# One fused layer on one core: the same stages in another hand-written order

## The reference

```
x = x + retention(layernorm(x))          # per sequence, 8 heads
  q, k rotated; v, g = x @ wv, x @ wg
  qk = (qr @ kr.T) * decay_mask;  qk = qk / clip(abs(qk.sum(-1)), 1)
  out = qk @ v;  out = out * rsqrt(mean(out^2));  out = (silu(g) * out) @ wo
x = x + ffn(layernorm(x))                # here the 8 sequences are the "time" axis
  attention over the sequences at the same position, 16 heads, 4 key/value heads, causal
  h1 = x + ao @ wproj;  x2 = layernorm(h1)
  router: softmax over 8 experts, the best 2, with a capacity of 640 tokens for each expert
  each expert: gelu(x2 @ w1[e]) @ w2[e], weighted and added to h1
```

## Time and profile before

| | |
|---|---|
| median of 3 runs | 232.73 us (232.41 to 233.09) |
| time of the profiled execution | 232.53 us |
| its span | 230.7 us |
| PE busy | 218.4 us (95% of the span) |
| DVE busy | 180.6 us (78%) |
| ACT busy | 148.6 us (64%), of it 48.8 us in 38 table loads |
| POOL busy | 87.5 us (38%) |
| granted clock of PE | 1.0 throughout |

### The profile page before, as it was taken

One profiled execution on the slowest core, in us unless ns is written; L12 is line 12 of the kernel. 1 busy time (PEld: TensorE's weight loads), 2 busy tenths in 40 slices (PEclk: granted clock), 3 DMA queues, 4 the chain that ended last, 5 costly groups with the idle time before them and its releaser, 6 DMA issues.

```text
span 230.7 us, 5045 instructions
## 1 busy us (share of the span) xinstructions
PE 218.4 (95%) x1794; PEld 185.6 (80%) x1794; DVE 180.6 (78%) x549; ACT 148.6 (64%) x274; POOL 87.5 (38%) x107
## 2 busy tenths in 40 slices
PE   7898897999998999999999999999999799989994
PEld 7577675888976879878989788968897789878994
DVE  2799968898998899789988997897479846875533
ACT  3648757789856589648874886559656574737331
POOL 0000243235274436346455752653197317701000
DMA  5994000000000000000000000000000000000000
GB/s 160 298 323 104 1 3 1 3 0 0 4 0 4 0 26 0 1 3 1 23 3 0 3 1 26 0 0 12 15 0 4 23 0 3 23 0 1 26 0 23
DMA packets 8072, 6.45 MB, mean 28 GB/s; under 512 B 752, under 2 KB 7152, under 8 KB 8048
## 3 DMA queue, kind: packets, MB, share of 16 engines
q1 hardware_dynamic: 8048, 6.14, 9.1%
HBM read 5.09 MB, written 1.05 MB: 27 GB/s over the span
## 4 chain that ended last, share of the span: by engine, by line
PE 59%; issue 12%; DVE 11%; POOL 9%; ACT 6%; DMA 1%; DVEq 0%; POOLq 0%; ACTq 0%
PE bankm L860 15%; PE bankm L849 15%; POOL prodv L325 5%; PE bankf L672 3%; PE bank L739 3%; PE bankf L680 3%; PE bankf L731 3%; ACT L480 3%; POOL prod L317 3%; PE bank L761 2%; PE bank L787 2%; DVE ao L1058 2%; PE bank L770 2%; PE bankf L689 2%; PE bankf L700 1%
## 5 line engine op out<-in xcount | busy, mean ns | idle before, releaser
L849 PE MATMUL bankm<-x2T,w 128*128 128x256 f32 x256 | 64.9, 386 | 1.9 <-DVE res L1165 1.7
L860 PE MATMUL bankm<-w,hT 128*128 128x128 f32 x512 | 64.9, 276 | 0.1
L860 PEld LDWEIGHTS bankm<-w,hT 128*128 128x128 f32 x512 | 62.1, 192 | 2.0 <-issue 0.8
L1165 DVE SCALAR_TENSOR_TENSOR res<-bankm,gate,res 128x128 f32<-128x128 f32 x128 | 38.3, 341 | 21.3 <-PE bankm L860 20.7
L628 ACT ACTIVATE hT<-bankm 128x512 f32<-128x512 f32 x64 | 37.5, 596 | 26.7 <-PE bankm L849 26.5
L849 PEld LDWEIGHTS bankm<-x2T,w 128*128 128x128 f32 x256 | 45.2, 190 | 10.0 <-DVE res L1165 4.3
L480 ACT ACT_TABLE_LOAD x38 | 48.8, 1283 | 1.4 <-PEq L1207 0.7
L317 POOL TENSOR_TENSOR prod<-qkv 128x384 f32<-128x384 f32 (+5 forms) x12 | 19.9, 1681 | 18.5 <-ACT qkv L490 18.5
L325 POOL TENSOR_TENSOR prodv<-attn_exp,qkv 128x384 f32<-128x384 f32 (+5 forms) x12 | 18.1, 1529 | 12.6 <-ACT attn_exp L596 12.6
L1058 DVE TENSOR_REDUCE ao<-prodv 128x128 f32<-128x256 f32 (+6 forms) x14 | 16.7, 1206 | 1.1 <-POOL prodv L325 0.9
L394 POOL TENSOR_TENSOR qk<-rot_a,rot_s 128x512 f32<-128x512 f32 x6 | 7.7, 1275 | 15.4 <-DVE rot_s L907 15.4
(11 more groups left out here) (129 smaller groups left out, 403.4 us busy)
## 6 DMA issues: line engine op xcount, KB each, us to landing
x<-in_x SPq DMA_DIRECT2D x8, 128.0 KB, 5.0
w<-in_w SPq DMA_DIRECT2D x1, 1024.0 KB, 6.0
out<-res SPq DMA_DIRECT2D x8, 128.0 KB, 1.8
con<-in_consts SPq DMA_DIRECT2D x1, 512.0 KB, 4.3
con<-in_consts SPq DMA_DIRECT2D x1, 256.5 KB, 4.3
con<-in_consts SPq DMA_DIRECT2D x1, 256.0 KB, 4.4
rcon<-in_rconsts SPq DMA_DIRECT2D x1, 132.0 KB, 2.8
wqk<-in_wqk SPq DMA_DIRECT2D x1, 128.0 KB, 3.4
```

Of the source, the lines that this page charges most:

```text
L849: last = mm(m_banks[n % NM][:, t * SLEN:(t + 1) * SLEN], w1[:, e, t * P:(t + 1) * P], x2T[:, i], start=True, stop=True)
L860: last = mm(m_banks[n % NM][:, c * D:(c + 1) * D], hT[:, n % NM, t, c * P:(c + 1) * P], w2[:, e, t], start=(t == 0), stop=(t == NF - 1))
L1165: eng.scalar_tensor_tensor(res[:, i, c], m_banks[n % NM][:, c * D:(c + 1) * D], gate[:, i, c, e:e + 1], res[:, i, c], ALU.mult, ALU.add).t ...
```

## The change

The list ORDER is replaced by another list of the same 876 names. The first 26 names, up to `a_kT:0`, are unchanged. From `a_kcum:0` (the first use of sequence 0's rotated k) on, names stand in other places; no function, buffer, semaphore or table set is touched, and the new list also changes 38 times from one table to the other. A few lines from the diff, of the part around sequence 0's router and of the part around sequence 7's output projection:

```diff
-c_base:0 a_qo:2 a_silu:2 a_x1:1 a_rowsums:2 c_core:0 a_stats:5 a_s2:2 c_T:0 a_aggr:4 b_stats:1 c_x2T:0
-a_scores:2 a_stats:6 b_aggr:1 a_aggr:5 b_sub:1 m_fc1_0:0 a_mask:2 b_rstd:1 c_logits:0 b_hid:1 a_out:2 c_best:0
...
+p_warm:21 c_rstd:0 p_warm:22 p_warm:23 a_knat:2 c_core:0 a_state_mm:2 a_og:1 c_T:0 a_kcum:2 a_wo:1 a_tanh:2
+a_state:2 a_qkc:2 c_x2T:0 a_silu:2 a_qo:2 c_logits:0 a_stats:5 a_rowsums:2 c_best:0 a_x1:1 m_fc1_0:0 c_where:0
...
```

## The result

The changed kernel takes 232.04 us (median of 7 runs, 231.86 to 232.62), the kernel before 232.74 us (median of 7, 232.41 to 233.09). The ratio of the means is 0.9973, 95% interval 0.996 to 0.9986: 0.27% faster. The medians are 0.70 us apart, the means 0.63, so the gain is about the 0.7 us that I called measurable, and the interval leaves out no change. The forecast was 231.7 us, range 230.7 to 233.3.

A forecast was written before the change was run, and what follows sets the result against it. PE bounds the kernel, busy 218.4 of 230.7 us. The terms -0.3 + 0.65 - 1.2 - 0.2 + 0 = -1.05 us took 232.53 to 231.5, plus 0.2 for the median: 231.7 us, range 230.7 to 233.3.

The forecast's parts named there:

- The router: Sequence 1's router: 1.2 us earlier, as c_onehot:1 on DVE no longer collides with a_og:3 on POOL.
- `a_qo:4` delays `a_og:3` by 0.5 us, so the one-hot gets in first by some 0.2 us: Sequence 1's router: c_onehot:1 reached after about 2.0 us, a_og:3 after about 2.2, both counted from the end of a_tt:3.
- The front: Start to the row sums of sequence 3: 0.3 us earlier, bounds 0 and 1.2, by filling two PE waits.
- I arrive at `a_qk:3` 0.5 us earlier: Front, sequence 3: PE reaches a_qk:3 0.5 us earlier, at 44.7 us, against 45.18 in the kernel before.
- `a_silu:3` gives 0.2 of it back: Front: a_silu:3 loses 0.2 us of the 0.5, with a_stats:7 and one more aggregation ahead of it on DVE.
- My sign of being wrong: Two-input DVE instruction meeting POOL ahead of an m_acc that PE awaits, or PE idle over 0.5 us between 72 and 142.
- Sequence 1's attention output: 0.65 us later, bounds +0.3 to +1.2: b_aoT_mm:1 waits 0.3 us, lost cover at a_T:4 and a_out:3 costs 0.35.
- The middle: Stretch from 72 to 142 us: 0.2 us earlier, bounds 0.3 earlier and 1.28 us later.
- The two forecast waits at `a_ms:6` and `a_state_mm:7`: Between 131 and 136 us: the new ACT order costs two waits of 0.5 us, but PE comes there 0.7 us earlier.
- The point from which I said ACT decides: Rival, ACT the bound at 131 to 136 us if a_tt:6 ends after 135.4: 233.3 us, chance 0.21.
- in the middle PE is the bound and an order can only lose: Premise for the middle: PE lacks only 0.1 us of the 70 between 72 and 142 us.
- Sequence 7's projection: Output projection: 0, bounds -0.9 and +0.3; the wait at b_aoT_mm:6 goes, c_T:6 gets one of about 0.8 us.

The follow-up runs named there:

- experiment 6: Changed kernel with b_prod:1 moved ahead of m_acc_0:0 and a_aggr:7 on DVE: 230.98 us, ratio 0.9928 to the kernel before.
- experiment 4: Kernel before with one stage moved on ACT, a_qo:4 ahead of a_rs:3: 231.83 us, ratio 0.9962.
- Experiment 5: Changed kernel with a_qo:4 moved back behind a_rs:3 on ACT: 232.7 us, ratio 1.0002 to the kernel before.
- Experiments 1: New order up to a_rowsums:3, then the order of the kernel before: 233.16 us, ratio 1.0014 to the kernel before.
- the same late part: New order from b_ao:4 (about 130 us) on, in the kernel before: 233.07 us; changed kernel with the old order there instead: 232.74 us.
- experiment 12: Changed kernel with b_prod:1 ahead of m_acc_0:0, and the order of before from c_aggr:5 on: 232.03 us, ratio 0.9968 to the kernel before.

## Why the prediction was right, and where it was not

**The router: right.** The step "`a_qo:4` delays `a_og:3` by 0.5 us, so the one-hot gets in first by some 0.2 us" held: 70.14 against 70.39, a lead of 0.25 us. The term was -1.2; the lag fell by 1.49 us there in the changed kernel, 1.48 in experiment 6, and 0.76 from `a_qo:4` alone in experiment 4. Half of the term is the one stage moved on ACT. Experiment 5 shows it from the other side: with `a_qo:4` back, 0.68 us of the fall is left. The other half, of which I had given 0.2 us to `a_wo:3` and `c_rank:1`, the runs don't divide. It does not come from the rise of 0.40 us just ahead, since experiment 6 has a rise of 0.11 us and the same fall.

**The front: wrong in sign.** "I arrive at `a_qk:3` 0.5 us earlier" held: 45.51 - 0.77 = 44.74, the 44.7 that was forecast. The step that failed is "`a_silu:3` gives 0.2 of it back". It gave 0.8 back. I had looked for the collision of DVE with POOL at the router alone, and walked `b_prod:1` with its old length of 1.27 us; in the new order it starts just behind `a_og:2`. My sign of being wrong asked only for a meeting ahead of an `m_acc`; this one stood ahead of `a_silu:3`. Experiments 1 and 6 show it from both sides. The Trainium skill (SBUF — State Buffer, section "SBUF: two separate sides") has the rule by which this could have been found, and the traces bear out both halves of it: DVE pays when POOL starts first (2.20 us in the changed kernel, 1.20 for 0.13 in experiment 5), POOL when DVE does (1.45 for 1.27 in experiment 6).

**Sequence 1's attention output: too dear.** I put +0.65 there; the lag rose by 0.40 us in the changed kernel and by 0.11 in experiment 6, where PE comes early as the prediction had it. No wait came up at `b_aoT_mm:1` in either.

**The middle: right within 0.15.** -0.2 was forecast for it all; it is -0.29 up to 128 us and +0.22 from there to 137. The two forecast waits at `a_ms:6` and `a_state_mm:7` are one of 0.24 us at the second, and `a_knat:7` ran at 135.41, 0.1 us behind the forecast of 134.5 once the late start is taken off:

```profile
134.88 0.63 ACT L552 ACTIVATE lt<-tt 128x512 f32<-128x512 f32 x1
135.41 0.25 ACT L490 COPY knat<-bankf 128x128 f32<-128x128 f32 x1
```

The point from which I said ACT decides was `a_tt:6` ending after 135.4 us; it ended at 134.36. One premise was wrong here: "in the middle PE is the bound and an order can only lose". From `a_scores:4` to `a_T:7` both kernels do the same products, and PE has no idle time over 0.1 us there in the kernel before. Yet it takes 48.44 us before and 48.21 in the changed kernel. So PE's busy time is not a fixed price of its work; what makes it shorter the runs don't show.

**Sequence 7's projection: right.** PE's timeline of the changed kernel, for the earlier trace rows:

```profile
179.52 0.44 PE L798 MATMUL bank<-con,aon 128*128 128x128 f32 x2
180.42 0.71 PE L806 MATMUL bank<-wproj,aoT 128*128 128x128 f32 x4 [0.46 <-ACT aoT L490]
...
183.66 0.44 PE L813 MATMUL bank<-con,core 128*128 128x128 f32 x2 [0.77 <-DVE core L1096]
```

The wait of 1.01 us is gone and one of 0.77 stands at `c_T:6`, as forecast (0.8). The lag moves by 0.02 us from 137 us to the end.

In sum: forecast -1.05, lag -0.73. The front was 0.7 us worse than forecast, router, attention output and middle together 0.4 us better. The prediction was right on the mechanism that decided; its front term was wrong and partly made up for.

## What to carry to other kernels

In an order by hand or by planner, the pairs to look for are two-input SBUF instructions of DVE that start just behind a long instruction of POOL. Here which of the two started first was worth about 0.8 us each time (experiments 4 and 6), and delaying the one that had slack was enough. Price a moved stage by what arrives late at its new place, not by the wait that it leaves, and do not add prices: the same late part cost 0.3 us alone and saved 0.4 us behind the new front. A junction of two good orders is a third order, and three of the eight here made a wait of their own.

## What the runs showed of the hardware

The start of the kernel varies from one execution to the next. Over the 14 profiled executions `a_state_mm:0` started between 10.60 and 12.02 us, and lists with the same names to that point start early (10.60, 10.73) and late (11.20, 12.02). PE's timelines in the changed kernel and then in experiment 6, whose lists are the same there:

```profile
5.48 1.06 PE L650 MATMUL bankm<-warm 128*128 128x128 f32 x4
6.33 1.33 PE L672 MATMUL bankf<-xT,wqk 128*128 128x256 f32 x4
```

```profile
5.12 0.61 PE L650 MATMUL bankm<-warm 128*128 128x128 f32 x4
5.74 1.13 PE L672 MATMUL bankf<-xT,wqk 128*128 128x256 f32 x4
```

The same four warm-up instructions (two `p_warm` stages) take 1.06 us in the one and 0.61 in the other, at a granted clock of 1.00 in both. In experiment 12, the latest start, PE then also waited 0.67 us for `wv` to land. What sets the pace of the first products isn't settled here. The runs of one kernel spread by 0.4 to 1.4 us. That the start is most of this spread is likely, since start and lag together give every profiled time, but it isn't shown: each kernel has one profile.
